# Local attention tiles: the product with the inverse norms moved from VectorE to GpSimd

## The reference

```python
qkv = shift_token(x) @ wqkv                       # 8 heads of 64
q, k = l2norm(q) * q_scale, l2norm(k) * k_scale   # norm per token and head
q = q * cos * scale + rotate_half(q) * sin * scale
k = k * cos / scale + rotate_half(k) * sin / scale
x = x + softmax(band(8 * q @ k.T)) @ v @ wo       # window of 64 tokens and the one before
h = layernorm(shift_token(x)) * ln_g + ln_b
a, g = split(h @ w1 + b1)
x = x + (a * gelu(g)) @ w2 + b2
```

## Time and profile before

| what | value |
|---|---|
| runs (3), median | 409.67 us |
| runs, lowest and highest | 408.95, 409.79 us |
| profiled execution, span | 406.5 us |
| profiled execution, its full time | not on the page |
| TensorE busy | 352.7 us (87%) |
| VectorE busy | 338.9 us (83%), 725 instructions |
| ScalarE busy | 295.9 us (73%) |
| GpSimd busy | 58.6 us (14%), 45 instructions |
| local tiles | from about 204 us to the end |

### The profile page before, as it was taken

How to read it: one execution, slowest core, us unless ns; L and a number is a source line. 1 busy time by engine, 2 the same in 40 slices (tenths; PEclk the granted TensorE clock), 3 DMA queues, 4 the chain that set the end, 5 groups by cost and what they waited for, 6 DMA issues and landing times.

```text
span 406.5 us, 10233 instructions
## 1 busy us (share of the span) xinstructions
PE 352.7 (87%) x4033; PEld 251.1 (62%) x4036; DVE 338.9 (83%) x725; ACT 295.9 (73%) x727; POOL 58.6 (14%) x45
## 2 busy tenths in 40 slices
PE   2899999999945878998798889999999999998676
PEld 1498888887731424555455556567676767676565
DVE  5989987887789889979679999989899999986343
ACT  1789999896434337776747787898989898986663
POOL 2000002000003021000023123403132323212110
PEclk9999999999985699999989999999999999999779
DMA  8800010000000000000000000000000000000001
GB/s 315 347 4 3 4 42 3 3 4 3 2 0 0 2 1 0 2 2 2 0 2 2 0 0 2 0 2 2 1 2 2 1 2 0 2 2 0 2 1 52
DMA packets 1774, 8.29 MB, mean 20 GB/s; under 512 B 192, under 2 KB 448, under 8 KB 1472
## 3 DMA queue, kind: packets, MB, share of 16 engines
q1 hardware_dynamic: 1728, 7.65, 4.8%
HBM read 7.12 MB, written 0.52 MB: 19 GB/s over the span
## 4 chain that ended last, share of the span: by engine, by line
PE 43%; DVE 29%; ACT 17%; issue 10%; DMA 1%; DVEq 0%; ACTq 0%
PE ps L252 15%; ACT PT L1525 5%; ACT blk L1411 3%; DVE PT L1232 3%; PE ps L506 3%; DVE lneg L1216 3%; PE ps L620 3%; DVE blk L1190 2%; DVE ss_floor L1200 2%; PE ps L656 2%; ACT PT L1595 2%; PE ps L379 2%; PE ps L493 2%; DVE Y L870 2%; PE ps L582 2%
## 5 line engine op out<-in xcount | busy, mean ns | idle before, releaser
L1724 POOL TENSOR_TENSOR blk<-blk 128x1024 f32<-128x1024 f32 x16 | 37.7, 2359 | 170.6 <-DVE blk L1194 170.6
L568 PE MATMUL ps<-w_f,full 128*128 128x512 f32 x96 | 48.2, 619 | 0.9 <-issue 0.9
L1525 ACT ACTIVATE PT<-ps,lneg 128x128 f32<-128x128 f32 x128 | 45.0, 377 | 5.3 <-DVE lneg L1216 5.3
L252 PEld LDWEIGHTS ps<-blk,st 128*128 128x128 bf16 x768 | 26.8, 98 | 3.8
L1045 DVE TENSOR_REDUCE mneg<-ps 128x4 bf16<-128x512 bf16 x32 | 22.0, 688 | 7.7 <-PE ps L357 7.4
L1525 ACT ACTIVATION_READ_ACCUMULATOR PT<-ps,lneg 128x1 f32 x128 | 27.9, 218 | 0.0
L252 PE MATMUL ps<-blk,rel 128*128 128x64 bf16 x768 | 27.6, 193 | 0.0
L252 PE MATMUL ps<-blk,st 128*128 128x64 bf16 x768 | 27.6, 193 | 0.0
L1582 ACT ACTIVATE PT<-ps 128x512 f32<-128x512 f32 x32 | 17.5, 595 | 13.2 <-PE ps L506 13.2
L1216 DVE TENSOR_REDUCE lneg<-ps 128x8 f32<-128x1024 f32 x16 | 19.6, 1223 | 8.6 <-PE ps L252 8.5
L1232 DVE TENSOR_TENSOR PT<-PT,lrec 128x512 f32<-128x512 f32 x32 | 25.3, 790 | 1.1
(11 more groups left out here) (234 smaller groups left out, 905.5 us busy)
## 6 DMA issues: line engine op xcount, KB each, us to landing
w_f<-f_dram SPq DMA_DIRECT2D x2, 1689.0 KB, 13.3
w_x<-l_dram SPq DMA_DIRECT2D x1, 774.0 KB, 5.9
w_f<-ffn_dram SPq DMA_DIRECT2D x1, 561.0 KB, 7.9
X<-x_dram SPq DMA_DIRECT2D x1, 512.0 KB, 3.6
ctxT<-ctxT_dram SPq DMA_DIRECT2D x1, 512.0 KB, 4.4
OT<-maskT_dram SPq DMA_DIRECT2D x1, 512.0 KB, 7.1
rest<-l_dram SPq DMA_DIRECT2D x1, 385.0 KB, 4.8
const<-const_dram SPq DMA_DIRECT2D x1, 324.0 KB, 6.3
```

The lines of the kernel that those rows point to most:

```text
L252: return mm(out, l, r, start=start, stop=False, skip_group_check=True)
L568: m = mm(ps[:, c, :], hT[:, n, :], w_f[:, l, F_QKV + 512 * c:F_QKV + 512 * (c + 1)], start=True, stop=True)
L1525: e = a(S1[:, i % 2, P * k:P * (k + 1)], ps[:, 3 + c, P * j:P * (j + 1)], ACT.Exp, bias=lneg[:, i % 2, k:k + 1], accum_out=lsum[:, i % 2, ...
L1724: g_.tensor_tensor(R[:, i % 2, :], R[:, i % 2, :], T2, ALU.add).then_inc(sem("pair_sum"), 1)
```

## The change

The work of `unit_norm` is split. VectorE keeps the Newton step under the name `head_rate`, with its three instructions now at L1206, L1208 and L1212, and signals `rate`. GpSimd gets the product (L1733), behind `sum_pairs` of the same tile (now L1727), and signals `rope`, for which TensorE's transpose waits as before. lr becomes a pair of buffers by the tile's parity, and the Newton step waits for the product two tiles back before it writes one. Below the place of the change, VectorE's and GpSimd's line numbers are higher by 3: L1216, L1229, L1232 and L1252 are now L1219, L1232, L1235 and L1255, and GpSimd's L1734 is L1750.

```diff
--- before.py
+++ after.py
@@ -175,7 +175,7 @@
         lss = sb("lss", [2 * LH])
         lr0 = sb("lr0", [2 * LH])
         lnt = sb("lnt", [2, 2 * LH])
-        lr = sb("lr", [2 * LH])
+        lr = sb("lr", [2, 2 * LH])
         lsum = sb("lsum", [2, LH])
         lrec = sb("lrec", [LH])
 
@@ -1201,13 +1201,16 @@
                 settle()
                 v.tensor_reduce(ss[:, :], ss_floor[:, :, :], AX.X, ALU.max).then_inc(sem("ss"), 1)
 
-            def unit_norm(i):
+            def head_rate(i):
                 dve.wait_ge(sem("root"), i + 1)
-                dve.wait_ge(sem("pair_sum"), i + 1)
-                newton(ss[:, :], lr0[:, :], lnt, lr[:, :])
-                r = R[:, i % 2, :].rearrange("p (h j) -> p h j", j=LD)
-                v.tensor_tensor(r, r, lr[:, :].rearrange("p (h o) -> p h o", o=1).to_broadcast([P, 2 * LH, LD]),
-                                ALU.mult).then_inc(sem("rope"), 1)
+                step(v.tensor_tensor(lnt[:, 0, :], lr0[:, :], lr0[:, :], ALU.mult))
+                settle()
+                step(v.scalar_tensor_tensor(lnt[:, 1, :], lnt[:, 0, :], -0.5, ss[:, :], ALU.mult, ALU.mult))
+                settle()
+                if i >= 2:
+                    dve.wait_ge(sem("rope"), i - 1)
+                v.scalar_tensor_tensor(lr[:, i % 2, :], lnt[:, 1, :], 1.5, lr0[:, :], ALU.add, ALU.mult)\
+                    .then_inc(sem("rate"), 1)
 
             def largest(i):
                 dve.wait_ge(sem("lscores"), i + 1)
@@ -1262,20 +1265,20 @@
             rotate(0)
             sum_squares(0)
             divide_batch(4)
-            unit_norm(0)
+            head_rate(0)
             divide_batch(5)
             rotate(1)
             sum_squares(1)
             largest(0)
             divide_batch(6)
-            unit_norm(1)
+            head_rate(1)
             for i in range(4):
                 if i >= 1:
                     largest(i)
                 if i == 0:
                     divide_batch(7)
                 if i >= 1:
-                    unit_norm(i + 1)
+                    head_rate(i + 1)
                 if i == 1:
                     normalise(6, X, Z, "z_in", 4, NB)
                 normalise_p(i, 0)
@@ -1723,11 +1726,24 @@
                 pool.wait_ge(sem("rotated"), i + 1)
                 g_.tensor_tensor(R[:, i % 2, :], R[:, i % 2, :], T2, ALU.add).then_inc(sem("pair_sum"), 1)
 
-            for i in range(4):
+            def unit_norm(i):
+                pool.wait_ge(sem("rate"), i + 1)
+                pool.wait_ge(sem("pair_sum"), i + 1)
+                r = R[:, i % 2, :].rearrange("p (h j) -> p h j", j=LD)
+                g_.tensor_tensor(r, r, lr[:, i % 2, :].rearrange("p (h o) -> p h o", o=1).to_broadcast([P, 2 * LH, LD]),
+                                 ALU.mult).then_inc(sem("rope"), 1)
+
+            sum_pairs(0)
+            unit_norm(0)
+            sum_pairs(1)
+            unit_norm(1)
+            for i in range(2, 4):
                 sum_pairs(i)
+                unit_norm(i)
             for q in range(8):
                 for i in range(4 + 2 * q, min(6 + 2 * q, 2 * NB)):
                     sum_pairs(i)
+                    unit_norm(i)
                 l, j = divmod(q, 4)
                 z, x = Z[:, 2 * j:2 * j + 2, :], X[:, 2 * j:2 * j + 2, :]
                 pool.wait_ge(sem("halves"), q + 1)
```

## The result

The changed kernel takes 415.65 us (median of 4 runs, 415.37 to 418.5) against 409.31 us before (4 runs, 406.56 to 409.79). The ratio is 1.0199, with a 95% interval of 1.0144 to 1.0254: slower by 6.3 us between the medians, and by 5.9 to 10.4 us by the interval. (A ratio here is taken over the runs and need not be the quotient of the two medians.) The forecast was 419.7 in a range of 413 to 424.

What follows compares the result with a forecast made beforehand. VectorE's place in the chain linking nearly full engines was taken to bound the kernel. Pairs 6.9, tile 14 0.9 and tiles 0 to 3 2.2 gave +10.0: span 416.5, with 3.1 around it 419.7 us, range 413 to 424.

Steps and rivals of the forecast that it cites:

- The mechanism: VectorE instructions with two SBUF inputs stand still until GpSimd's instruction is through; those with one or a PSUM input go on.
- The product's price: GpSimd's product of 1024 elements per partition taken at 2.36 us, like its sum; range 1.23 to 2.83.
- Even tiles: L877 held until GpSimd's product ends, making VectorE's L879, rows and rotation later: +0.94 us each.
- Odd tiles: First L1232 held to 0.55 us after GpSimd's product, so the second and L1252 come later: +0.43 us each.
- The sign named for a failing sum: TensorE having the chain in tiles 0 to 3, where it gets its operand 1.2 us later, would fail the sum.
- Tile 1: Has an even tile's order, Newton step and four rows, so the same hold: +0.94 us.
- Tile 14: Last tile with a product; TensorE already waited 1.29 us for its rows, so the hold is paid in full: +0.9 us.
- Around the span: Time outside the profiled span, 3.1 us, from the runs' median of 409.67 against the span of 406.5.
- What a measurement can tell: A measurement of this kernel was taken to tell about 0.2%, 0.8 us, from no change.
- Rival B: The layer norm's small instructions slip past GpSimd's product, only odd tiles lose: 412.6 us; chance 0.08.
- The rule weighed there: One-SBUF-input instructions like L870 may be held too: same 10 us in the forecast, 417 us under rival B.
- Rival C: Nothing on VectorE is held by GpSimd's product: -0.7 us, time 409.0; chance 0.06.

Runs made afterwards that it cites:

- even_steps: Changed kernel with the product on GpSimd only where issued in even steps (tiles 5, 7, ... 15), the others on VectorE: 416.25 us, ratio to before 1.0193.
- the memset kernel: Kernel before plus a GpSimd memset of 1860 elements per partition, beside the Newton step in steps 4 to 14, read by nobody: 408.63 us, ratio 1.0035.
- rows_first: Changed kernel with VectorE doing the layer norm's Newton step and rows ahead of head_rate in even tiles: 408.3 us, ratio to before 1.0002.

## Why the prediction was right, and where not

- **The mechanism** held at every place named: L877 of the layer norm held to the end of GpSimd's product, L875 getting by, the first division of odd tiles ending 0.55 us after the product, handover in 0.08 us. One half of its premise did not hold, that an instruction with a single SBUF input goes on: L870 is held (1.08 us in tile 12), while the reciprocal in the odd tile isn't (0.18). The sign was right and the time inside the range, but the forecast lies 4 us above the measured median, and a pair takes 23.34 us where 23.7 to 23.8 was named. Without the clock the steps of the table lose 0.5 + 3.8 + 1.35 + 1.2 = 6.8 us, against a sum of 10.0.
- **The product's price** failed as a term: 1.90 us, not 2.36. No row of before showed a repeated factor at this size. The product also multiplies where the sum adds, and no run separates the two, so which of them makes it cheaper is open. The range had both ends, 1.23 and 2.83; I took the row of the same size, and the answer lay between.
- **Even tiles:** +0.94 forecast, +0.95 measured, and right for a wrong reason. The product holds for 0.46 less than I took, and the bias that the change puts behind it holds L879 for 0.48 more. The rows of the order ahead of the prediction show the bias behind the product; the sum had no term for it. Every GpSimd instruction behind the moved one should have been priced. With the residual in tile 12 it was 1.35.
- **Odd tiles:** +0.43 forecast, 0.0 measured. This is the 1.90 again: the held division ends 294.06, and the exponentials release the second only for 294.20. 2.36 would have ended 0.46 later and been on the chain, as worked out. With tiles 0, 2 and 3, which behave alike, that is 3.4 us of the sum that did not come. The sign named for a failing sum, TensorE's later operand in tiles 0 to 3, did not show: L582 starts 0.72 us later after the maximum in tiles 0 and 2, and their steps are unchanged.
- **Tile 1:** +0.94 forecast, +0.5 measured; the same 0.46, and no bias there. That is the even tile's term without its accident.
- **Tile 14:** +0.9 forecast, 1.2 of hold measured (the residual is in it), and 1.7 of clock, for which the sum had no term.
- **Around the span:** 3.1 taken, 1.8 measured. That is 1.3 us of the error. The 3.1 set the median of the runs against the span of another execution.
- **What a measurement can tell** was put at 0.2%, from three runs. The later runs of the kernel before, 29 to a set, lie between 405.4 and 411.2 us, and the interval of the result is 0.55% to either side.
- **Rival B** was half right in the race: in even_steps one small instruction more slipped through, and the next was caught. The rule weighed there (the Trainium skill, "SBUF — State Buffer", Who interferes with whom: `tensor_scalar` can take both ports) is borne out by L870's 1.08 us beside the residual. The same section of the Trainium skill says that a GpSimd instruction which only writes doesn't hold two-input instructions; the memset kernel agrees, at 0.17 us for L877.
- **Rival C** put the gain without any hold at 0.7 us. No run is free of holds and has the product at VectorE's price. rows_first comes nearest: no gain in its pairs (22.38 us against 22.40), and both the rotation's wait for the square and the division's for the exponentials are there in its profile, as C had it.

So the sign and the place of the loss were read rightly, and that the time came out within 4 us owes something to errors that offset each other: in the even tiles almost exactly, and over the span 2.8 us of clock in tile 14 and behind it against 2.0 ahead of the tiles. What stays open is why the clock dips behind tile 14's wait in some executions and not in others with about the same wait (1.29 us before, 1.30 with the memset), and whether a longer wait makes it likelier. No run held the clock fixed.

## What to carry to other kernels

Before work goes from VectorE to GpSimd, list what VectorE does for the length of the GpSimd instruction and of those queued behind it there. In these traces an instruction of VectorE with two SBUF inputs that met a reading GpSimd instruction stood until that one was through, be it on two numbers (1.89 us in place of 0.16), and one like L870 can too. One that reads PSUM lost nothing (the rotation, 1.23 us beside the product), nor did a reduction (the maximum, 1.21 to 1.23 us beside the rotation sum). Order the handover so that the second kind comes next, and look for such holds that are there already: a wait on GpSimd that avoids one gained 2.7 us by the medians here, of which 1.4 shows in the steps, and the moved product gained nothing in any order tried.

## What the runs showed of the hardware that was not expected

- A GpSimd product whose second factor is repeated 64 times along the row takes 1.90 us for 1024 elements (1.899 to 1.904, 16 times), the sum of two full tensors 2.36.
- GpSimd's copy of 1548 elements takes 1.47 us and its memset of 1860 elements 1.65: per element that is 0.95 and 0.89 ns, against 2.3 for the sum of two tensors. Reading one input costs little there by these figures; the second is the dear one.
- The same 50 TensorE instructions behind tile 14's wait took 6.41 us at a clock of 1.00 and 8.1 to 8.2 us at 0.79, and the kernel with the memset had the slow stretch behind the same 1.3 us of waiting as the kernel before.
